# A mixture-of-experts stage reordered: one expert's row list inside its neighbour's inner product, both row turns between the outer products

## The chip, the cores and the metric

One Trainium2 chip, and of it one core. The metric is the device time of one launch in microseconds (us), shown as the median of three runs. Beside it stands one profiled execution, from which all rows below come. TensorE is called PE here, VectorE DVE, ScalarE ACT, GpSimd POOL and SyncE SP, as in the profile.

## What is computed

The reference is a two-layer model on 625 nodes with 768 features. Each layer adds to `x` a graph part and a feed-forward part, each on the layer norm of `x`:

```
x = x + gat(layernorm(x))                   # 10000 edges, 8 heads, then 1 head
x = x + moe_ffn(layernorm(x)) + spectral    # 8 experts, all of them on all rows
x = x + rgcn_and_gcn(layernorm(x))          # 34 relations, 768x768 weights each
x = x + routed_experts(layernorm(x))        # the stage that is changed
```

The last part is

```
logits = flat @ Wr;  probs = softmax(logits);  topk_p, topk_i = top_k(probs, 2)
capacity = ceil(625 * 2 / 8 * 1.25) = 196
order  = argsort(-score, axis=1)[:, :capacity]     # per expert: the 196 best rows
gate, up = silu(flat[order] @ w1), flat[order] @ w3          # 768 -> 192
out    = scatter_add((gate * up) @ w2 * weight) + silu(flat @ s1) * (flat @ s3) @ s2
```

so that there is one shared expert over all 625 rows (five tiles of 125) and eight routed experts with 196 rows each, in two halves of 98.

## The kernel before, in words

The kernel is one program with five queues that are written out by hand; every wait on a semaphore is in the text, and the order in a queue is the order of execution. Three stretches matter here.

**The relation stage.** For each of 34 relations a one-hot list (`in_list`, DVE) picks rows; PE turns the list into row numbers (`list_rows`), POOL gathers rows by them, PE turns the rows and multiplies them by the relation's weights, which ACT and DVE have split into a high and a low part (`w_high`, `w_low`). `in_list` of relation r+3 stands in the DVE queue of relation r, behind `w_low` of relation r+1; PE's `list_rows` of it stands ahead of the products of relation r+1.

**The shared expert.** PE makes five inner products (`shared_inner`; the first three carry eight more columns with the router's logits, and `last_logits` makes those of tiles 3 and 4 by themselves), turns the hidden rows (`shared_turn`) and makes five outer products (`shared_outer`). DVE adds each of these straight from PSUM to the residual `x_res` (`add_shared`), between pieces of its ranking work. ACT computes silu (`shared_gate`), the router's exp (`router(2)`) and the copies (`shared_turned`).

**The routed experts.** For expert e, in this order:

- PE spreads the scores of all rows over the partitions (`score_spread(e)`, five transposes into PSUM slot 3), ACT copies them out (`score_row(e)`), DVE ranks every row against them (`rank(e)`, with fourteen compare-and-sum instructions) and writes the one-hot list (`placed(e)`).
- PE multiplies the list by the row numbers (`list_places(e)`, ten narrow matmuls into slot 0), DVE reads the numbers (`rows2(e)`), POOL issues two gathers of 98 rows each from DRAM into `fx`.
- PE turns both halves (`turn_x(e, 0)` and `turn_x(e, 1)`, both into slot 0, so that the second waits until ACT's `take_x` has emptied it), makes the inner product in three parts of 12 matmuls (gate in two parts, then up), and two outer products of 8 matmuls (`outer_product(e, 0)` and `(e, 1)`), whose results ACT writes out (`y_out`) and stores to `y_dram`.
- SP loads the weights of expert e as soon as the inner product of expert e-3 (`w13`) and its outer products (`w2e`) are done, in a ring of three.

In the loop before, PE's queue for expert e from 2 on is: inner product e; first turn of e+1; first outer product of e; second turn of e+1; spread e+4; a wait for `x_taken` of both halves of e+1; `list_places(e+2)`; second outer product of e. So a row list is made two experts ahead of its use. `turn_hots(0)` and `turn_hots(1)`, which turn the last expert's one-hot list, come in the loop at experts 5 and 6.

**The end.** The rows of experts 0 to 5 that a node needs are gathered back from `y_dram` (`y_lower`) and added with their weights (`add_lower`, five DVE instructions, placed before the last expert's `hidden_rest`), those of a second choice likewise (`y_higher`, `add_higher`); the last expert's result is split in two parts (`y_last` on ACT, `last_low` on DVE) and multiplied by the one-hot lists (`join`, PE), DVE adds the result (five instructions), and SP stores each tile.

## Time and profile before

| | us |
|---|---|
| runs (three) | 1416.32, 1418.84, 1422.12 |
| median | 1418.84 |
| profiled execution, own time | 1422.75 |
| its span in the profile | 1421.2 |
| mean granted PE clock, share of full | 0.953 |
| PE busy in the span | 1303.6 (92%) |
| DVE busy | 964.3 (68%) |
| POOL busy | 649.2 (46%) |
| ACT busy | 557.1 (39%) |

The span is what the profiler saw of the one execution, some 1.6 us less than that execution's own time. Granted clock 1.00 is 2.4 GHz, 0.50 is 1.2 GHz. A busy PE is not PE at its peak: a stretch at the lower clock counts as busy too.

### The profile page before, as it was taken

What the parts mean: (1) busy time and instruction counts of PE and PEld (TensorE: products, weight loads), DVE (VectorE), ACT (ScalarE), POOL (GpSimd) and SP (SyncE); (2) the same over time, 40 slices, a digit from 0 to 9 for tenths busy, and PEclk for the clock granted to TensorE, in tenths of its full rate; (3) what the DMA queues carried; (4) which work ended last, traced back from release to release, by engine and by line L of the source; (5) the groups of instructions that cost most, each with busy time, mean ns of one, the idle gap of its engine ahead of it and who ended that gap; (6) DMA issues with size and microseconds to landing.
All of it is one profiled execution on the core that took longest, in us unless ns stands there. A gap on an engine that the chain in (4) does not pass through costs nothing.

```text
span 1421.2 us, 22852 instructions
## 1 busy us (share of the span) xinstructions
PE 1303.6 (92%) x7540; PEld 1103.8 (78%) x7540; DVE 964.3 (68%) x2158; ACT 557.1 (39%) x652; POOL 649.2 (46%) x564
## 2 busy tenths in 40 slices
PE   7988678999999989999999999999999879988997
PEld 5765568656996779999999999999866569656665
DVE  8967899888689645565656565656158875477634
ACT  0010476232433044555555555555147761212221
POOL 7025777767677633344434443544178740011121
PEclk9999697999999899999999999999999999989998
DMA  6940000020740347878787878787579863415645
GB/s 172 91 46 6 2 2 1 2 68 1 208 107 2 91 156 253 291 251 298 253 304 258 297 255 298 263 293 246 142 248 328 271 211 89 129 41 161 169 133 167
DMA packets 116402, 234.59 MB, mean 165 GB/s; under 512 B 36930, under 2 KB 57086, under 8 KB 116300
## 3 DMA queue, kind: packets, MB, share of 16 engines
q1 hardware_dynamic: 80780, 126.83, 31.0%
q0 software_dynamic: 22352, 70.40, 17.7%
q10 hardware_dynamic: 13200, 36.46, 6.9%
q8 instruction: 39, 0.64, 0.2%
q14 instruction: 31, 0.25, 0.1%
HBM read 195.26 MB, written 39.70 MB: 165 GB/s over the span
## 4 chain that ended last, share of the span: by engine, by line
PE 64%; DVE 21%; issue 5%; DMA 4%; ACT 3%; POOL 1%; DVEq 0%; ACTq 0%; SPq 0%; POOLq 0%
PE PS L2725 28%; PE PS L2599 4%; PE PS L2388 4%; PE PS L2713 3%; PE PS L3010 3%; PE PS L2674 3%; PE PS L2788 3%; DVE e L1321 3%; PE PS L2900 2%; PE PS L2999 2%; PE PS L2858 2%; DVE mlo L2163 2%; DVE e L1563 2%; DVE e L1600 1%; DMA pre<-z_dram,grow 1%
## 5 line engine op out<-in xcount | busy, mean ns | idle before, releaser
L815 POOL DMA_INDIRECT xg<-xn_dram,xrow x70 | 111.7, 1596 | 270.0 <-DVEq L1530 248.2
L2725 PE MATMUL PS<-whi,xhi 128*128 128x384 f32 x840 | 220.8, 343 | 1.0 <-ACTq L1103 1.0
L2725 PE MATMUL PS<-whi,xlo 128*128 128x384 f32 x840 | 215.0, 337 | 0.0
L2725 PE MATMUL PS<-wlo,xhi 128*128 128x384 f32 x840 | 213.5, 335 | 0.0
L1321 DVE TENSOR_TENSOR wlo<-raw,whi 128x2304 fp32r<-128x2304 f32 x68 | 175.2, 2576 | 39.6 <-ACTq L1086 33.7
L1084 ACT ACTIVATE whi<-raw 128x2304 fp32r<-128x2304 f32 x68 | 145.1, 2134 | 27.3 <-DMA raw<-in_L_gnn_W_rel 11.6
L2725 PEld LDWEIGHTS PS<-wlo,xhi 128*128 128x128 f32 x840 | 152.0, 188 | 0.0
L2725 PEld LDWEIGHTS PS<-whi,xlo 128*128 128x128 f32 x840 | 151.9, 188 | 0.0
L2725 PEld LDWEIGHTS PS<-whi,xhi 128*128 128x128 f32 x840 | 148.5, 189 | 1.3 <-issue 1.3
L1321 DVE TENSOR_TENSOR xlo<-PS,xhi 128x768 fp32r<-128x768 f32 x70 | 67.0, 958 | 121.6 <-ACTq L1095 114.3
L785 POOL DMA_INDIRECT zidxb<-zrow_dram,idxb x80 | 110.9, 1386 | 25.7 <-issue 25.7
L783 POOL DMA_INDIRECT evwb<-inv_dram,idxb x80 | 106.6, 1333 | 30.5 <-issue 22.4
L801 POOL DMA_INDIRECT edge_dram<-recb,idxb x80 | 97.1, 1214 | 39.5 <-issue 21.4
L1101 ACT ACTIVATE xn<-PS 128x768 f32<-128x768 f32 x70 | 56.8, 812 | 145.5 <-PE PS L2725 131.2
L1094 ACT ACTIVATE xhi<-PS 128x768 fp32r<-128x768 f32 x70 | 56.9, 813 | 86.6 <-issue 53.6
L2388 PE MATMUL PS<-onehot 125*128 125x347 bf16 (+6 forms) x640 | 74.8, 261 | 10.7 <-DVE onehot L1387 10.7
L884 POOL DMA_INDIRECT fx<-xn_dram,xrow x16 | 15.5, 971 | 141.1 <-DVEq L2251 138.6
L2388 PEld LDWEIGHTS PS<-onehot 125*128 125x128 bf16 x640 | 53.8, 99 | 27.4 <-issue 10.7
L2858 PE MATMUL PS<-mhi,hotf 128*125 128x384 f32 x170 | 59.7, 433 | 16.7 <-DVE mlo L2163 11.2
L2491 PE MATMUL PS<-hx,e 125*125 125x97 f32 x350 | 51.9, 323 | 15.2 <-DVE e L1600 15.2
L859 POOL DMA_INDIRECT pre<-z_dram,grow x45 | 56.7, 1260 | 16.8 <-issue 8.8
L2491 PEld LDWEIGHTS PS<-hx,e 125*125 125x125 f32 x350 | 51.0, 238 | 16.2 <-issue 16.2
(463 smaller groups left out, 2652.0 us busy)
## 6 DMA issues: line engine op xcount, KB each, us to landing
raw<-in_L_gnn_W_rel SPq DMA_DIRECT2D x68, 1152.0 KB
z_dram<-xn ACTq DMA_DIRECT2D x70, 384.0 KB, 7.3
gw<-in_L_gnn_W SPq DMA_DIRECT2D x2, 2304.0 KB, 27.1
fw<-in_L_ffn_w SPq DMA_DIRECT2D x8, 576.0 KB
fw<-in_L_ffn_w ACTq DMA_DIRECT2D x1, 4608.0 KB
y_dram<-yb ACTq DMA_DIRECT2D x14, 294.0 KB
xn_dram<-xn SPq DMA_DIRECT2D x10, 384.0 KB
wroot<-in_L_ffn_w SPq DMA_DIRECT2D x5, 576.0 KB, 4.9
```

Of the source, the lines that this page charges most:

```text
L783: pool.indirect_dma_start(evwb[:, n:n + 1], None, inv_dram, bass.IndirectOffsetOnAxis(ap=idxb[:, 0, n:n + 1], axis=0)).then_inc(evw_loaded ...
L785: pool.indirect_dma_start(zidxb[:, n:n + 1], None, zrow_dram, bass.IndirectOffsetOnAxis(ap=idxb[:, 1, n:n + 1], axis=0)).then_inc(rows_loa ...
L801: pool.indirect_dma_start(edge_dram, bass.IndirectOffsetOnAxis(ap=idxb2[:, k:k + 1], axis=0), recb[:, k, :], None, bounds_check=T * GE - 1 ...
L815: pool.indirect_dma_start(xg[b][j][:, :], None, xn_dram, bass.IndirectOffsetOnAxis(ap=xrow[:, b, j:j + 1], axis=0)).then_inc(x_gathered[b] ...
L1084: step.do(act.activation(whi[b][:, half * KH:(half + 1) * KH, :], raw[:, half * KH:(half + 1) * KH, :], ACT.Copy))
L1094: step.do(act.activation(xhi[b][j][:, :, :], columns_of(j), ACT.Copy))
L1321: return dve.tensor_tensor(o, a, b, op)
L2388: pe.matmul(PS[:, c:c + m], onehot[:, b, i * 128:(i + 1) * 128], onehot[:, b, HOT_REL + o:HOT_REL + o + m], start=start and c % BANK == 0, ...
L2491: mm = pe.matmul(slot(3)[0:P, b * BANK + i * (HC + 1):b * BANK + (i + 1) * (HC + 1)], e2[b][:, t, i * P:(i + 1) * P], hx[:, t, h * (HC + 1 ...
L2599: mm = pe.matmul(o[0:end, :, :], w[:, k, 0:end], xs[:, t0:t1, k, 0:TW], start=(k == 0 and part == 0), stop=(k == K - 1 and part == 2), ski ...
L2725: mm = pe.matmul(slot(q)[:, s * BANK:s * BANK + HALF], a[:, k, :], wt[:, k, s * HALF:(s + 1) * HALF], start=(k == 0 and part == 0), stop=( ...
L2858: mm = pe.matmul(slot(MSG_SLOT[n][0])[0:P, s * BANK:s * BANK + HALF], hotf[q % 4][:, 0:P], part[:, s * HALF:(s + 1) * HALF], start=False, ...
```

## The change

All changes are in the order of work, in two PSUM slots and in waits; the same sums are formed, the adds in another order.

- PE: `list_places(e+1)` is now made inside the inner product of expert e, between the gate parts and the up part; for every expert the queue is inner product, spread e+3, first outer product, both turns of e+1, second outer product. `turn_x(e, 0)` writes slot 0 and `turn_x(e, 1)` slot 3 (`X_SLOT`), and the waits for `x_taken` ahead of the turns and the list are gone. A row list is thus made one expert ahead, and a score row three ahead. Both `turn_hots` are in expert 6.
- DVE: `rank` and `placed` of expert n+2 behind `hidden_first(n)`; `add_shared` reads SBUF and is moved to after `row_tables`, `add_lower` to after the last `hidden_first`.
- ACT: copies the shared outer products out of PSUM (`shared_out`, into the buffer `xn`, once its five stores to DRAM have landed), and makes one exp of a column of ones ahead of the router's.
- PE, shared expert: the logits of tiles 3 and 4 behind `shared_inner(1)` and `shared_inner(2)`; `shared_outer(0)` ahead of the first spread.
- SP: the load of `w13` for expert e waits for the rows of expert e-2 as well.
- Relation stage: the one-hot list of relation 3 is made before the stage and not in its first turn.

```diff
-SPREAD_AHEAD = 4
+SPREAD_AHEAD = 3
+X_SLOT = (0, 3)
+SHARED_SLOT = (0, 1, 2, 1, 2)
...
             for e in range(RING, NE):
                 sp.wait_ge(inner_full, SH + 3 * (e - RING + 1))
+                for k in range((e - RING + 1) * RT, (e - RING + 2) * RT):
+                    sp.wait_ge(x_gathered[k % 4 // 2][k % 2], 16 * (REL // 2 + (k % 2 == 0) + k // 4 + 1))
                 load_w13(e, e % RING, ld_w13[e % RING])
...
+            def shared_out(t):
+                act.wait_ge(outer_full, t + 1)
+                step.do(act.activation(xn[:, t, :].rearrange("p (b c) -> p b c", b=2),
+                                       slot(SHARED_SLOT[t]).rearrange("p (b c) -> p b c", c=BANK)[0:P, :, 0:HALF], ACT.Copy))
+                act.sem_inc(outer_taken, 1)
+
             for t in range(LOGITS_WITH):
                 shared_gate(t)
+            act.activation(table_of_exp[:, :], ones[0:P, 0:1], ACT.Exp)
             shared_turned(0)
             router(2)
             shared_gate(3)
             shared_turned(1)
+            score_row(0)
+            act.wait_ge(xn_stored, 32 * T)
+            shared_out(0)
             shared_gate(4)
-            score_row(0)
             shared_turned(2)
+            shared_out(1)
             shared_turned(3)
+            shared_out(2)
             score_row(1)
+            shared_out(3)
             shared_turned(4)
-            score_row(2)
+            shared_out(4)
...
             for n in range(NE):
                 expert_gates(n)
+                if n == 0:
+                    score_row(2)
+                if n + SPREAD_AHEAD < NE:
+                    score_row(n + SPREAD_AHEAD)
+                if n == FINAL - 1:
                     for j in range(RT):
+                        hot_out(j)
...
                 y_out(n, 0)
+                for j in range(RT):
+                    take_x(n + 1, j)
                 y_out(n, 1)
...
-            in_list(2, 0)
+            for b in range(2):
+                in_list(2 + b, b)
...
             def add_shared(t):
+                dve.wait_ge(outer_taken, t + 1)
+                do(tt(x_res[:, t, :], xn[:, t, :], x_res[:, t, :], ALU.add))
...
+            for n in range(NE):
                 hidden_rest(n)
+                if n + 1 < NE:
+                    rows2(n + 1)
                 hidden_first(n)
                 if n + 2 < NE:
+                    rank(n + 2, 0, T)
+                    placed(n + 2)
+                elif n + 2 == NE:
                     row_tables()
+                    for t in range(T):
+                        add_shared(t)
...
+            dve.wait_ge(y_lower_gathered, 16 * T)
+            for t in range(T - 1):
+                add_lower(t)
+            last_low(0)
+            add_lower(T - 1)
             add_higher(0)
             last_low(1)
+            for t in range(1, T):
+                add_higher(t)
...
             def turn_x(e, j):
...
-                if k:
-                    pe.wait_ge(x_taken, k)
+                if j == 1 and e == FINAL:
+                    pe.wait_ge(hots_ready, RT)
+                elif j == 1:
+                    pe.wait_ge(srow_ready, min(e + SPREAD_AHEAD, NE) if e else 2)
...
+            for e in range(NE):
+                def between():
+                    if e + 1 < NE:
+                        list_places(e + 1)
+                    if e == 0:
+                        score_spread(2)
+                    if e == FINAL - 1:
+                        turn_hots(0)
+
+                inner_product(e, between)
                 if e + SPREAD_AHEAD < NE:
                     score_spread(e + SPREAD_AHEAD)
+                if e == FINAL - 1:
+                    turn_hots(1)
+                outer_product(e, 0)
+                if e < FINAL:
+                    for j in range(RT):
+                        turn_x(e + 1, j)
                 outer_product(e, 1, 0 if e == FINAL else 2)
```

## Rows read from the trace of the kernel before

**Rows 1.** Windows: stretch, length, busy by engine (instructions), clock, DMA share, GB/s

```profile
1266.90:1390.60 123.70, 110.15 (x553) 76.76 (x553) 67.29 (x295) 29.27 (x48) 18.31 (x19) 0.90 0.55 153
...
1342.75:1359.69 16.94, 15.42 (x76) 10.34 (x75) 9.89 (x43) 3.60 (x6) 1.94 (x2) 0.90 0.64 175
...
1376.90:1390.62 13.72, 13.55 (x70) 9.67 (x69) 1.04 (x4) 4.29 (x7) 4.75 (x5) 1.00 0.61 198
```

**Rows 2.** Timeline of PE, experts 4 to 6: start, us, line, idle before it

```profile
1349.60 2.99 PE L3010 MATMUL PS<-w2e,hidden 128*98 128x384 f32 x8
1352.52 0.72 PE L2985 MATMUL PS<-ident,fx 98*128 98x98 f32 x6
1354.66 0.62 PE L2965 MATMUL PS<-node_of,inlist 125*98 125x2 bf16 x10 [1.42 <-ACTq L1229]
1355.14 4.62 PE L3010 MATMUL PS<-w2e,hidden 128*98 128x384 f32 x8
1359.69 6.24 PE L2999 MATMUL PS<-fxT,wroot 128*128 128x196 f32 x36
...
1387.73 2.96 PE L3010 MATMUL PS<-pre,hidden 128*98 128x384 f32 x8
```

**Rows 3.** Windows around two falls of the clock, columns as in the first group

```profile
1232.60:1236.00 3.40, 3.40 (x7) 1.85 (x6) 1.46 (x9) 3.07 (x4) 0.00 (x0) 0.50 0.95 255
...
1355.50:1358.90 3.40, 3.40 (x6) 1.26 (x5) 3.02 (x13) 0.00 (x0) 1.94 (x2) 0.50 0.34 98
```

**Rows 4.** Timeline, row gathers of POOL and a weight load of SP

```profile
1259.49 0.97 POOL L884 DMA_INDIRECT fx<-xn_dram,xrow  x1 [0.30 <-issue]
...
1274.72 1.55 SPq L688 DMA_DIRECT2D pre<-in_L_ffn_w  x3
...
1356.10 0.97 POOL L884 DMA_INDIRECT fx<-xn_dram,xrow  x1 [14.70 <-DVEq L2251]
```

**Rows 5.** Chain that ended last: start, us, of two gathers up to landing

```profile
1276.05 6.79 DMA fx<-xn_dram,xrow
...
1397.32 5.01 DMA pre<-y_dram,yrow
```

**Rows 6.** Timeline of DVE: rank and list of expert 2; `row_tables`; first and last

```profile
1275.87 0.87 DVE L2227 TENSOR_SCALAR_CACHE_REDUCE compared<-srow,scol 125x625 f32<-125x625 f32 x1 [0.17 <-DVE xrow L2250]
...
1284.73 0.99 DVE L2242 TENSOR_SCALAR inlist<-iota,poscol 125x196 bf16<-125x196 int16 x5
...
1372.76 0.20 DVE L1321 TENSOR_TENSOR ysel<-asg,rev 125x40 f32<-125x40 f32 x1
...
1377.06 0.20 DVE L2289 TENSOR_REDUCE yw<-ysel 125x5 f32<-125x40 f32 x1
```

**Rows 7.** Timeline from behind the logits to the first inner product, all engines

```profile
1232.29 5.73 PE L2909 MATMUL PS<-pre,xT 128*125 128x384 f32 x12
...
1232.97 1.28 ACT L1025 ACT_TABLE_LOAD   x1
...
1241.94 0.71 PE L2426 MATMUL PS<-ident,scol 125*125 125x125 f32 x5
...
1247.99 2.06 DVE L1321 TENSOR_TENSOR x_res<-PS,x_res 125x768 f32<-125x768 f32 x2
...
1255.87 0.59 PE L2965 MATMUL PS<-node_of,inlist 125*98 125x2 bf16 x10 [1.91 <-DVEq L2244]
...
1266.89 7.80 PE L2999 MATMUL PS<-fxT,pre 128*128 128x196 f32 x36 [0.84 <-issue]
```

**Rows 8.** Timeline of PE and DVE, ahead of and in the relation stage

```profile
507.69 0.96 DVE L1321 TENSOR_TENSOR x_res<-PS,x_res 125x768 f32<-125x768 f32 x1 [5.92 <-PE PS L2695]
...
539.50 0.41 PE L2472 MATMUL PS<-node_of,inlist 125*128 125x2 bf16 x10 [2.97 <-DVEq L1513]
...
613.43 0.40 PE L2472 MATMUL PS<-node_of,inlist 125*128 125x2 bf16 x10 [1.32 <-DVEq L1513]
```

**Rows 9.** Timeline, the end: the last add

```profile
1414.39 1.02 DVE L2361 SCALAR_TENSOR_TENSOR x_res<-PS,comb,x_res 125x768 f32<-125x768 f32 x1 [0.39 <-PE PS L3076]
```

More of the change, by code:

```diff
@@ L1227, in take_x @@
                 act.wait_ge(turned, n * RT + j + 1)
-                step.do(act.activation(fxT[n % 2][:, :, j * HT:(j + 1) * HT], columns2(0)[:, :, 0:HT], ACT.Copy))
+                step.do(act.activation(fxT[n % 2][:, :, j * HT:(j + 1) * HT], columns2(X_SLOT[j])[:, :, 0:HT], ACT.Copy))
                 act.sem_inc(x_taken, 1)
@@ L2021, in x_low, with relation @@
                 dve.sem_inc(xlo_ready, 1)
-            def relation(i, b, listed, more):
+            def relation(i, b, listed, more, list_coming=True):
                 if more:
@@ L2030, in relation @@
                     w_low(i + b, 1 - b, 0, 1)
-                if listed:
+                if listed and list_coming:
                     in_list(i * 2 + b + 3, 1 - b)
@@ L2041, in _ @@
             for b in range(2):
-                relation(0, b, True, True)
+                relation(0, b, True, True, b == 1)
             with dve.Fori(1, REL // 2 - 2) as i:
@@ L2261, in hidden_first, with add_lower @@
                 dve.sem_inc(h2_ready, 1)
-            def add_lower():
-                dve.wait_ge(y_lower_gathered, 16 * T)
-                for t in range(T):
-                    step(dve.scalar_tensor_tensor(x_res[:, t, :], y_lower[t][0:P, :], yw[:, 0, t:t + 1], x_res[:, t, :], ALU.mult, ALU.add))
-                step.sync()
+            def add_lower(t):
+                do(dve.scalar_tensor_tensor(x_res[:, t, :], y_lower[t][0:P, :], yw[:, 0, t:t + 1], x_res[:, t, :], ALU.mult, ALU.add))
             def row_tables():
@@ L2294, in _ @@
             shared_hidden(3)
-            shared_hidden(4)
             dve.wait_ge(earlier_ready, 1)
             rank(0, 0, 3)
-            add_shared(0)
-            add_shared(1)
+            shared_hidden(4)
             rank(0, 3, T)
             placed(0)
-            add_shared(2)
             rows2(0)
-            rank(1, 0, 2)
-            add_shared(3)
-            rank(1, 2, 4)
-            add_shared(4)
-            rank(1, 4, T)
-            placed(1)
-            hidden_rest(0)
-            hidden_first(0)
-            rows2(1)
-            rank(2, 0, T)
-            placed(2)
-            rank(3, 0, 3)
-            hidden_rest(1)
-            rows2(2)
-            hidden_first(1)
-            rank(3, 3, T)
-            placed(3)
-            rank(4, 0, 3)
-            rows2(3)
-            rank(4, 3, T)
-            placed(4)
+            rank(1, 0, T)
+            placed(1)
             do(dve.tensor_copy(ident16[:, :], ident[0:P, 0:P]))
-            for n in range(2, NE):
-                if n == FINAL:
-                    add_lower()
+            for n in range(NE):
                 hidden_rest(n)
+                if n + 1 < NE:
+                    rows2(n + 1)
                 hidden_first(n)
-                if n + 3 < NE:
-                    rank(n + 3, 0, 3)
                 if n + 2 < NE:
-                    rows2(n + 2)
-                if n + 3 < NE:
-                    rank(n + 3, 3, T)
-                    placed(n + 3)
-                elif n + 3 == NE:
+                    rank(n + 2, 0, T)
+                    placed(n + 2)
+                elif n + 2 == NE:
                     row_tables()
+                    for t in range(T):
+                        add_shared(t)
             def add_higher(t):
@@ L2911, in shared_inner, with logits_alone @@
                 mm.then_inc(inner_full, 1)
-            def last_logits():
+            def logits_alone(t):
                 pe.wait_ge(free[3], BEFORE["slot3"][3])
-                for t in range(LOGITS_WITH, T):
-                    pe.wait_ge(xT_ready, XT_TURNED[5] + t + 1)
-                    c = (t - LOGITS_WITH) * NE
-                    for k in range(K):
-                        mm = pe.matmul(slot(3)[0:P, c:c + NE], xT[:, k, t * P:(t + 1) * P], s13[:, k, 2 * F:2 * F + NE],
-                                       start=(k == 0), stop=(k == K - 1))
-                mm.then_inc(full[3], 1)
+                pe.wait_ge(xT_ready, XT_TURNED[5] + t + 1)
+                c = (t - LOGITS_WITH) * NE
+                for k in range(K):
+                    mm = pe.matmul(slot(3)[0:P, c:c + NE], xT[:, k, t * P:(t + 1) * P], s13[:, k, 2 * F:2 * F + NE],
+                                   start=(k == 0), stop=(k == K - 1))
+                if t == T - 1:
+                    mm.then_inc(full[3], 1)
             pe.wait_ge(split_lo, 2 * REL + SPLITS1 + K // 2)
@@ L2932, in _ @@
                 shared_inner(t)
[L2933 removed]
+                logits_alone(t + LOGITS_WITH - 1)
             def shared_turn(t):
@@ L3016, in _ @@
             shared_turn(1)
-            shared_inner(4)
+            shared_outer(0, 0)
             pe.wait_ge(hT_ready, 2)
@@ L3026, in _ @@
             shared_outer(2, 2)
+            pe.wait_ge(outer_taken, 1)
+            list_places(0)
             pe.wait_ge(hT_ready, 4)
```

61 lines of the change are left out of this document (3 added, 58 removed).

## The prediction, as made before the changed kernel ran

> **What bounds the kernel now.** I read the windows by stage first, then the timeline of PE in the expert stage, then the other queues at the places where PE waits. Between the first expert's inner product (1266.9) and the last one's (1390.6) lie 123.7 us, of which PE is busy for 110.2, at a mean granted clock of 0.90 [rows 1]. So PE bounds the stage, but loses time in two ways: 13.5 us idle, and part of the busy time at 1.2 GHz.
>
> One expert in the middle takes 16.94 us; expert 6, where PE does not wait for a list, 13.72 [rows 1]. The timeline shows the difference. After the first outer product (2.99 us) and the second turn, PE idles for 1.42 us until ACT has taken both halves, makes the list, and then needs 4.62 us for the same eight matmuls that take 2.96 where there was no such wait [rows 2]. The granted clock in that stretch is 0.50, the lower of the two levels [rows 3]. This comes once in each of experts 2 to 5, and costs 1.4 + 1.65 = 3.1 us where the wait is 1.42.
>
> Before the first expert, a chain over DVE's ranking sets the pace: PE waits 1.91 us for the first list at 1255.87, and the first inner product begins at 1266.89 [rows 7].
>
> **The change, part by part.** I walk through the queues with the durations of the rows.
>
> *One expert in the steady state.* The inner product takes 6.24 us, with the list (0.48 from its start to the next start) 6.72 [rows 2]. The hidden rows need another 0.6 before the outer product can start (13.72 less 6.24, two outer products of 2.9 and three short steps leaves no more); there a turn was hidden, now the spread of 0.71 [rows 7] is. So the first outer product starts 7.3 after the inner one, the first turn at 7.3 + 2.92 = 10.25. A turn takes about 0.6 with what follows it: the second could start at 10.8, the second outer product at 11.4, the next expert at 14.3.
>
> The new wait is for rows, since the list is now made for the next expert. It starts at 4.1 (24 of 36 matmuls). From there to the first gather are 1.44 us (1354.66 to 1356.10) [rows 2, 4], and the second gather follows 1.3 later (0.97 and 0.30) [rows 4]. Landing: a gather of 125 rows took 5.01 from issue, one of 98 rows beside a weight load 6.79 [rows 5]. I take 5.0, since the weights now start behind the rows; bounds are 4.3 (an estimate: 98 of 125 rows, by the share of the time that scales) and 6.8. With 5.0 the second half lands at 4.1 + 1.44 + 1.3 + 5.0 = 11.8, PE waits 1.0 us ahead of the second turn, and the next expert starts at 11.8 + 0.56 + 2.92 = 15.3; with 4.3 it is 14.6, with 6.8 it is 17.1. I take 15.2. Behind that wait stand the second turn, the second outer product and the next inner product, so that each us of it is one of the stage.
>
> Does the clock stay up? Before the fall at 1355.5 PE had a turn (0.7), an idle of 1.42 and the narrow list (0.6) [rows 2, 3], 2.6 us between the wide products. Now the list lies between wide matmuls, and two turns with the wait between them are left, about 2.1 us. Expert 6, with a turn and the one-hot turn back to back, kept 1.00 [rows 1]. Mine lies between; I take no fall, and price it as rival A.
> The Trainium skill (TensorE: Matmul & The Clock Gate, Part 4: PE-mode transpose) says that a transpose does not count as PE work in the way that a matmul does. By that, two turns with a wait between them are one quiet stretch, and the sum would be that of rival A. No row here shows turns alone.
>
> *DVE.* Rank and list of one expert take 9.85 us (1275.87 to 1285.72) [rows 6]. They start at 7.7 and the list is wanted 4.1 into the next expert, 15.2 + 4.1 - 7.7 = 11.6 later: 1.8 us of slack, so no cost; past that each us is one of PE. The five `add_shared` (1.03 each [rows 7]) leave the ranking chain. They now stand behind the tables of expert 6 (4.5 us, 1372.76 to 1377.26 [rows 6]) and ahead of `hidden_rest(7)`: done at 7.7 + 4.5 + 5.2 = 17.4, needed at 15.2 + 2.5. Just hidden.
>
> *The way to the first expert.* (1) Behind the logits alone, 24 matmuls of 8 columns, the clock falls and the fourth tile's inner product takes 5.73 us; 3.4 of that at 0.50 cost 1.7 [rows 3, 7]. Split into two pieces between wide products, I expect no fall: -1.7. (2) The first spread, at 1241.94, now waits for an outer product (2.9) and not for an inner one (5.73 - 1.7 = 4.0): -0.9. (3) Two adds (2.06) leave the first ranking, a small product (0.4) comes in [rows 7]: -1.7. The first list is thus made at 1251.5 and not 1255.87. Behind it PE has a spread (0.7), two outer products (2.9 each; ahead of the second, 1.0 of waiting, because ACT's new `shared_out(3)` stands ahead of the copy that it needs) and two turns. The second gather, 3.6 after the list as before (1255.87 to 1259.49 [rows 4, 7]), lands 5.0 later at 1260.1; then a turn and ACT's take lead to the inner product at about 1261.8, against 1266.89: -5.1. With the clock falling as before it is -3.4. (4) The exp of ones puts the router's table load (1.28 us [rows 7]) ahead of the need; its result comes 1 us sooner, but the spread waits for PE. I count nothing.
> The Trainium skill (ScalarE: Activation LUTs, What ACT_TABLE_LOAD costs) gives about 2.66 us with the drain for a switch of tables. A load of that length would end about 1234, a us later than needed, still ahead of the spread.
>
> *The first expert* begins after two turns and an idle of over 1 us, as before, and I leave it the slow start (7.80 for 6.24 [rows 2, 7]): 15.2 + 1.6, and a few tenths for the second spread inside it, 17.0 us.
>
> From the first inner product to the last: 17.0 + 6 x 15.2 = 108.2, against 123.7 [rows 1]: -15.5.
>
> *SP's wait.* The weights for expert e+3 now start some 12 us into expert e and are wanted over 30 us later; 1.2 MB at the stage's mean of 153 GB/s [rows 1] are 8 us. No cost. It removes what stood around the 6.79: weights issued at 1274.72, the gather at 1276.05 [rows 4, 5].
>
> *The end.* DVE bounds it. From 6.9 after the last inner product's start it has 5 lower, 5 higher and 5 last adds at 1.0 to 1.05 and two low parts of 0.96: 24.4, against 24.8 (1390.6 to 1415.4) [rows 9]. The lower rows are now issued behind the tables of expert 6 and land some 5.9 into the last expert, just before 6.9. -0.4.
>
> *Relation stage.* PE waited 2.97 us for the one-hot list of relation 3 [rows 8], which is now there: at most -3.0. But the chain of weight load, split and list runs close behind PE, which waits for it again at 613.43, 1.32 us [rows 8], and PE's lead may be given back there. Bounds 0 and -3.0; I take -2.0. The extra `in_list` ahead of the stage, 2 to 3 us, is followed by a DVE idle of 5.92 [rows 8], which hides it.
>
> **Sum.** -5.1 - 15.5 - 0.4 - 2.0 = -23.0. The profiled execution took 1422.75 us, so 1399.8 by its own time; the median of the runs is 3.9 lower, and from there 1418.84 - 23 = 1396.
>
> **The rivals.**
>
> *A. The clock still falls once per expert.* For it speaks the 1 us wait between the turns; against it, that the list has left that stretch. 1.65 x 6 = +9.9, with 1.7 at the logits +11.6: 1406 to 1408. Chance 0.20.
>
> *B. The rows come late, and the kernel is slower than before.* Gather latency is now on PE's path. Over seven experts, with the falls of A, the gain left is 23 - 9.9 = 13.1; it is used up once the second half lands 1.9 us later than I take, 6.9 from issue (the row beside a weight load has 6.79 [rows 5]). If the stores of `y_out`, the tail of a weight load and the other half's gather stretch it to 8.5, the sum is +11: 1430. Against it: the load is issued behind the rows and is over before the next gather. Chance 0.05.
>
> *C. The gain is swallowed by other waits*: DVE's 1.8 us of slack is not there, ACT's longer queue holds the start, the relation part gives 0. Within 7 us of before, about 1415. Chance 0.07.
>
> My own case has 0.68, with a range of its own of 1389 to 1403: rows after 4.3 us give -4 more, a relation stage with all 3 us another -1, a fast first expert -1.6; the relation part at 0, the fall at the logits and rows after 5.5 us give +7. 0.5% of this time is 7 us, about what a measurement of this kernel can tell from no change. The range over the cases is 1389 to 1410. Faster by over 0.5%: 0.88; within it: 0.07; slower: 0.05.
>
> **What would show it.** Right: starts of inner products 15.2 us apart; no outer product of 4.6 us; 0.5 to 1 us of idle ahead of the second turn, put down to the DMA into `fx`; the first inner product 5 us earlier after the logits, and none of 5.7 us behind them; no wait at the list of relation 3. Wrong: a clock of 0.50 once per expert (A); waits above 2 us at the turns (B); PE waiting for DVE at the list inside the inner product, or for ACT in the shared part (C); a wait for a list near 570 us that takes back the relation part.

## The result, and the profile after

Four runs of the changed kernel beside four of the kernel before gave 1405.31 us (1399.95 to 1408.58) against 1419.62. The medians are 14.3 us apart; the ratio on record is 0.988, 95% interval 0.986 to 0.990, which is 17 us (14 to 20). A second set (e1 below, with its own runs of the kernel before) gave 0.9876 (0.9848 to 0.9903), its medians 18.7 us apart. The forecast was 1396, with a range of 1389 to 1410. The profiled execution took 1404.76 us, its span 1403.0, at a mean granted clock of 0.955. Of the runs below, one of the twelve of e11 took 3233 us, more than twice the others, and is not in its ratio.

First the windows of the expert stage after: from the first to the last inner product, expert 4, expert 5 (columns as in [rows 1]).

```profile
1268.30:1372.40 104.10, 101.71 (x558) 73.28 (x558) 66.97 (x284) 29.96 (x49) 16.46 (x17) 0.98 0.58 167
1326.34:1340.88 14.54, 14.36 (x81) 10.39 (x80) 10.05 (x44) 4.30 (x7) 1.94 (x2) 1.00 0.71 205
1340.90:1357.90 17.00, 15.42 (x75) 10.40 (x74) 12.05 (x54) 3.61 (x6) 1.93 (x2) 0.90 0.56 159
```

123.7 us have become 104.1. The idle of 13.5 us is down to 2.4, and the clock went from 0.90 to 0.98 [rows 1]. By expert, from one inner product's start to the next, they were 23.7, 17.4, 17.9, 16.9, 16.9, 17.2 and 13.7 us before, and are 14.7, 14.4, 14.4, 14.6, 14.5, 17.0 and 14.5. So 8.9 of the 19.6 us come from the first expert alone. Before, PE waited in it for the rows of expert 1, which landed 6.79 us after issue beside the weights [rows 5], and a slow outer product (4.50 us) came behind. This line is from the kernel before:

```profile
1282.88 1.24 PE L2985 MATMUL PS<-ident,fx 98*128 98x98 f32 x6 [4.58 <-DMA fx<-xn_dram,xrow]
```

The timeline of PE after shows expert 4 and the end of expert 5; the rows beside it are POOL's second gather and SP's next weights in expert 4.

```profile
1326.34 4.25 PE L2984 MATMUL PS<-fxT,wroot 128*128 128x196 f32 x24
1330.42 0.58 PE L2948 MATMUL PS<-node_of,inlist 125*98 125x2 bf16 x10
1330.86 2.24 PE L2984 MATMUL PS<-fxT,wroot 128*128 128x196 f32 x12
1332.93 0.71 PE L2409 MATMUL PS<-ident,scol 125*125 125x125 f32 x5
1333.68 2.99 PE L2995 MATMUL PS<-w2e,hidden 128*98 128x384 f32 x8
1336.61 1.59 PE L2970 MATMUL PS<-ident,fx 98*128 98x98 f32 x12
1338.03 2.92 PE L2995 MATMUL PS<-w2e,hidden 128*98 128x384 f32 x8
...
1352.87 1.06 PE L2970 MATMUL PS<-ident,fx 98*128 98x98 f32 x6 [1.00 <-DMA fx<-xn_dram,xrow]
1353.72 4.26 PE L2995 MATMUL PS<-w2e,hidden 128*98 128x384 f32 x8
```

```profile
1333.09 0.97 POOL L889 DMA_INDIRECT fx<-xn_dram,xrow  x1 [0.30 <-issue]
...
1337.50 1.80 SPq L691 DMA_DIRECT2D wroot<-in_L_ffn_w  x3
```

The list lies between wide matmuls, and of what stood between the outer products in [rows 2] only two turns are left, 1.59 us for 1.18 where no row was awaited (at 1265.55 below): a wait of 0.4. SP's load, which waits for the rows, starts 4.41 us after the second gather's issue, which I take for the landing. (Where PE waited for such rows in experts 0 to 4 of e5 to e8, its turn began 4.4 to 4.7 us after the issue.) Only in expert 5 does PE wait a whole 1.00 us, and there the outer product is slow (4.26). The chain that ended last has that gather:

```profile
1347.63 5.19 DMA fx<-xn_dram,xrow
```

Then the way to the first expert, PE's timeline, against [rows 7]. The shared part begins at 1219.36 here and at 1216.21 before, so 3.15 are to be taken off.

```profile
1235.44 4.04 PE L2892 MATMUL PS<-pre,xT 128*125 128x384 f32 x12
...
1254.32 0.96 PE L2948 MATMUL PS<-node_of,inlist 125*98 125x2 bf16 x10 [2.03 <-DVEq L2252]
1255.14 1.39 PE L2409 MATMUL PS<-ident,scol 125*125 125x125 f32 x5
1256.33 5.04 PE L2934 MATMUL PS<-pre,hhT 96*125 96x384 f32 x8
1261.20 0.38 PE L2924 MATMUL PS<-ident,shh 125*96 125x125 f32 x2
1262.87 2.85 PE L2934 MATMUL PS<-pre,hhT 96*125 96x384 f32 x8 [1.28 <-ACTq L1278]
1265.55 1.18 PE L2970 MATMUL PS<-ident,fx 98*128 98x98 f32 x12
```

The window around them (columns as in [rows 1]):

```profile
1254.00:1261.00 7.00, 6.68 (x23) 4.54 (x24) 3.88 (x16) 0.69 (x1) 1.98 (x2) 0.51 0.27 69
```

The list of expert 0 comes 4.7 us earlier in relation to the shared part. But behind it the clock falls to 0.51, the outer product takes 5.04 us, and PE waits 1.28 us for ACT. The first inner product (1268.27) gains only 1.8.

In the relation stage the list of relation 3 waits for nothing, and the next one for 2.03 us:

```profile
537.54 0.40 PE L2455 MATMUL PS<-node_of,inlist 125*128 125x2 bf16 x10
553.85 0.40 PE L2455 MATMUL PS<-node_of,inlist 125*128 125x2 bf16 x10 [2.03 <-DVEq L1524]
```

At the end of the kernel DVE waits for the gathered lower rows (`y_lower`) and starts its lower adds 8.5 us after the last inner product's start:

```profile
1380.93 3.12 DVE L2272 SCALAR_TENSOR_TENSOR x_res<-wroot,yw,x_res 125x768 f32<-125x768 f32 x3 [1.80 <-DMA fx<-y_dram,yrow]
```

By stages the two traces differ by: ahead of the relation stage + 1.2, relation stage - 2.4, message stage (from PE's last wait in the relation stage to the first product of the GCN; the same code in both) + 4.3, way to the first expert - 1.8, experts - 19.6, end 0.0 (30.6 us from the last inner product's start, in both). That is - 18.3; the spans differ by 18.2.

### The profile page after: what moved, and what is told of

Its sections match the earlier page's. It is cut to its first block, busy times and chain, and to the rows that moved or that the text cites. A ratio compares the mean times of both kernels' runs of the same rounds, so it can differ in the third digit from the quotient of the medians.

```text
span 1403.0 us, 22858 instructions
## 1 busy us (share of the span) xinstructions
PE 1297.3 (92%) x7540; PEld 1104.0 (79%) x7540; DVE 965.0 (69%) x2158; ACT 560.5 (40%) x658; POOL 640.8 (46%) x564
## 4 chain that ended last, share of the span: by engine, by line
PE 62%; DVE 21%; issue 8%; DMA 4%; POOL 2%; ACT 2%; DVEq 0%; SPq 0%; another core or an unknown queue 0%; ACTq 0%; POOLq 0%
PE PS L2708 30%; PE PS L2582 4%; PE PS L2371 4%; PE PS L2696 3%; PE PS L2520 3%; PE PS L2657 3%; PE PS L2771 3%; DVE e L1332 3%; PE PS L2883 2%; PE PS L2841 2%; DVE e L1574 2%; DVE e L1611 2%; DVE mlo L2175 2%; DMA pre<-z_dram,grow 1%; PE PS L2803 1%
## 5 line engine op out<-in xcount | busy, mean ns | idle before, releaser
L820 POOL DMA_INDIRECT xg<-xn_dram,xrow x70 | 107.1, 1530 | 282.8 <-DVEq L1541 249.8
L1089 ACT ACTIVATE whi<-raw 128x2304 fp32r<-128x2304 f32 x68 | 145.1, 2134 | 26.1 <-DMA raw<-in_L_gnn_W_rel 14.2
L788 POOL DMA_INDIRECT evwb<-inv_dram,idxb x80 | 108.7, 1359 | 30.5 <-issue 22.4
L806 POOL DMA_INDIRECT edge_dram<-recb,idxb x80 | 101.0, 1263 | 39.5 <-issue 22.5
L2841 PE MATMUL PS<-mhi,hotf 128*125 128x384 f32 x170 | 63.5, 458 | 17.1 <-DVE mlo L2175 15.5
L889 POOL DMA_INDIRECT fx<-xn_dram,xrow x16 | 15.5, 971 | 128.4 <-DVEq L2259 125.9
L2474 PE MATMUL PS<-hx,e 125*125 125x97 f32 x350 | 53.0, 327 | 16.9 <-DVE e L1611 16.9
L2474 PEld LDWEIGHTS PS<-hx,e 125*125 125x125 f32 x350 | 52.2, 243 | 17.9 <-issue 17.9
L2841 PEld LDWEIGHTS PS<-mhi,hotf 128*125 128x125 f32 x170 | 31.7, 210 | 43.7 <-DVE mlo L2175 29.6
```

The costliest lines, as they stand in the source:

```text
L788: pool.indirect_dma_start(evwb[:, n:n + 1], None, inv_dram, bass.IndirectOffsetOnAxis(ap=idxb[:, 0, n:n + 1], axis=0)).then_inc(evw_loaded ...
L806: pool.indirect_dma_start(edge_dram, bass.IndirectOffsetOnAxis(ap=idxb2[:, k:k + 1], axis=0), recb[:, k, :], None, bounds_check=T * GE - 1 ...
L820: pool.indirect_dma_start(xg[b][j][:, :], None, xn_dram, bass.IndirectOffsetOnAxis(ap=xrow[:, b, j:j + 1], axis=0)).then_inc(x_gathered[b] ...
L1089: step.do(act.activation(whi[b][:, half * KH:(half + 1) * KH, :], raw[:, half * KH:(half + 1) * KH, :], ACT.Copy))
L2474: mm = pe.matmul(slot(3)[0:P, b * BANK + i * (HC + 1):b * BANK + (i + 1) * (HC + 1)], e2[b][:, t, i * P:(i + 1) * P], hx[:, t, h * (HC + 1 ...
L2841: mm = pe.matmul(slot(MSG_SLOT[n][0])[0:P, s * BANK:s * BANK + HALF], hotf[q % 4][:, 0:P], part[:, s * HALF:(s + 1) * HALF], start=False, ...
```

## The experiments

Twelve kernels ran, in five rounds beside the kernel before: e1 to e4 on one chip, e5 to e8 on a second, e9 to e12 on a third. The kernel before is not equally fast on them (1411.8, 1421.4, 1422.0 us), so times are compared within a chip, and across chips only by ratio. "Start" is the time from the first inner product of the shared part to that of expert 0, "experts" that from the first to the last expert's inner product, both from the run's profile.

| run | median, before | ratio (95%) | start | experts |
|---|---|---|---|---|
| before | | | 50.7 | 123.7 |
| changed, first set | 1405.3, 1419.6 | 0.988 (0.986 to 0.990) | 48.9 | 104.1 |
| e1 the same | 1393.1, 1411.8 | 0.9876 (0.9848 to 0.9903) | 45.7 | 101.9 |
| e2 weights ahead | 1414.7, 1411.8 | 1.0030 (1.0006 to 1.0054) | 49.0 | 122.7 |
| e3 list late | 1429.8, 1411.8 | 1.0136 (1.0114 to 1.0158) | 47.4 | 139.4 |
| e4 relation old | 1395.0, 1411.8 | 0.9885 (0.9858 to 0.9911) | 49.0 | 101.4 |
| e5 logits together | 1406.1, 1421.4 | 0.9883 (0.9857 to 0.9910) | 47.3 | 102.4 |
| e6 adds in ranking | 1402.2, 1421.4 | 0.9869 (0.9843 to 0.9896) | 49.7 | 101.7 |
| e7 turned first | 1399.8, 1421.4 | 0.9841 (0.9816 to 0.9866) | 44.9 | 102.3 |
| e8 front | 1401.5, 1421.4 | 0.9844 (0.9819 to 0.9870) | 50.0 | 102.4 |
| e9 list in the middle | 1401.5, 1422.0 | 0.9853 (0.9816 to 0.9891) | 48.3 | 100.7 |
| e10 turn ahead | 1419.3, 1422.0 | 0.9982 (0.9958 to 1.0006) | 45.7 | 119.8 |
| e11 one slot | 1426.8, 1422.0 | 1.0023 (0.9991 to 1.0055) | 48.2 | 121.9 |
| e12 outer first | 1399.9, 1422.0 | 0.9845 (0.9808 to 0.9883) | 45.6 | 102.6 |

**e1, the changed kernel again.**

> The changed kernel once more, unaltered, as the measure for the runs beside it. In its first profile the experts from the first to the last inner product took 104.1 us, the first inner product came only 1.8 us earlier relative to the shared part, and the message stage, whose code is the same in both kernels, took 144.9 us against 140.6 before, at a clock of 0.91 against 0.96. If that is chance of the single execution, this profile has the message stage nearer to 141 and the ratio is 0.985 to 0.990; if the change itself slows that stage, it is near 145 again. Expert 5 alone was late (17.0 us for 14.5): if its place is chance, it moves or goes.

The code is that of the first profile, and start and experts differ all the same: the outer product behind the list took 2.75 us and not 5.04, and expert 5 waited 0.81 us without a slow outer product. The message stage took 162.1 us here, against 164.7 before and 169.0 in the first profile. Over all thirteen profiles of changed kernels it took 157.3 to 171.2, and it goes with the chip: 157.3 to 162.1 in e1 to e4, 164.6 to 167.1 in e5 to e8, 165.7 to 171.2 in e9 to e12. So the + 4.3 lies within what the same code shows on one chip (5.5 us in e9 to e12) and says nothing of the change; and most of the 10 us by which the first of these chips is faster lies in this stage.

**e2, the weights ahead of the rows.**

```diff
-                for k in range((e - RING + 1) * RT, (e - RING + 2) * RT):
-                    sp.wait_ge(x_gathered[k % 4 // 2][k % 2], 16 * (REL // 2 + (k % 2 == 0) + k // 4 + 1))
                 load_w13(e, e % RING, ld_w13[e % RING])
```

> The next weights are issued as soon as the inner product is over, as in the kernel before, and no longer behind the rows. My account: the load runs beside the gathers, which then land 6.8 us after issue (row of the kernel before) and not 4.5; PE waits about 2.4 us ahead of the turns of experts 1 to 5, the clock falls in the outer product behind (1.65 us each): + 10 to + 20 us against the changed kernel, ratio 0.995 to 1.002. Rival: the rows don't suffer from the load, and the wait is worth nothing: within 3 us of the changed kernel.

+ 21.7 us by the medians, just over the upper end, and the kernel is now 0.3% slower than before. In the profiles the experts account for + 20.8. Expert 2, PE and the second gather on POOL:

```profile
1302.08 0.72 PE L2968 MATMUL PS<-ident,fx 98*128 98x98 f32 x6
1305.48 1.24 PE L2968 MATMUL PS<-ident,fx 98*128 98x98 f32 x6 [2.68 <-DMA fx<-xn_dram,xrow]
1306.52 4.90 PE L2993 MATMUL PS<-w2e,hidden 128*98 128x384 f32 x8
```

```profile
1298.57 0.97 POOL L887 DMA_INDIRECT fx<-xn_dram,xrow  x1 [0.30 <-issue]
```

The rows are there 6.9 us after issue, as the row of before had it (6.79 [rows 5]). The five experts that issue a load took 18.6, 16.9, 19.5, 20.0 and 18.4 us, the two without one 14.8 and 14.6. The waits of those five are 2.2 to 2.7 us, as expected, and the clock fell behind three of them (outer products of 3.9 to 5.6 us). The rival falls: SP's wait, to which the prediction gave no gain of its own beyond the landing, is worth as much as the whole gain of the change (18.7 us on this chip), since without it the rest brings nothing.

**e3, the list behind the up part.** The only edit besides is that DVE's `rows2` follows `hidden_first`.

```diff
-                    if e + 1 < NE:
-                        list_places(e + 1)
...
                 inner_product(e, between)
+                if e + 1 < NE:
+                    list_places(e + 1)
```

> The list of the next expert is made behind the last part of the inner product and not ahead of it, so that its rows are asked for 2.1 us later. My account: the landing of the rows is on PE's path with next to no slack (0.1 to 0.4 us of waiting per turn), so each of seven experts loses about 2 us of waiting and, since the turns are then apart, the clock falls in the outer product behind them (1.65 us): + 14 to + 25 us against the changed kernel, ratio 0.998 to 1.006. Rival: there is slack, and PE's own work sets the 14.5 us of an expert: + 0 to + 4 us.

+ 36.8 us, more than I allowed. PE in expert 2:

```profile
1308.97 1.24 PE L2970 MATMUL PS<-ident,fx 98*128 98x98 f32 x6 [1.39 <-DMA fx<-xn_dram,xrow]
1310.98 1.24 PE L2970 MATMUL PS<-ident,fx 98*128 98x98 f32 x6 [0.77 <-DMA fx<-xn_dram,xrow]
1312.01 4.74 PE L2995 MATMUL PS<-w2e,hidden 128*98 128x384 f32 x8
```

The waits are 1.7 to 2.6 us an expert, about as expected. The clock's part is the larger one: 139.4 - 101.9 = 37.5 over seven experts is 5.4 each, so about 3 go to the lower clock. The outer product behind the turns is slow in all seven (3.9 to 5.6 us), and the next inner product in four of them (7.55 us at 1275.53, for 6.24).

**e4, the relation list as before.**

```diff
-            for b in range(2):
-                in_list(2 + b, b)
+            in_list(2, 0)
...
-                relation(0, b, True, True, b == 1)
+                relation(0, b, True, True)
```

> The one-hot rows of relation 3 are made inside the relation loop again, as in the kernel before; all else is changed. My account: + 2.4 us against the changed kernel, with the wait of 3 us ahead of the list of relation 3 back, and the later wait of 2 us gone. Rival: the later stages give the lead back, and it is within 1 us.

+ 1.9 us by the medians, within the intervals, so the times don't settle it. The trace is plainer: from the outer product before the stage (503.86 here, 503.44 in the kernel before) to the product behind PE's last wait in it there are 514.0 us, the same as in the kernel before (513.9), against 511.7 in e1 beside it and 508.9 to 513.8 in the twelve profiles with the new order at this place (mean 511.5). The first list waits 3.06 us again and the second not at all. How much the new order gains goes with its own second wait: where that was 0.6 to 1.4 us (e2, e6, e7, e9) the stage took 508.9 to 509.7, where it was 2.6 to 2.9 (e5, e8, e10, e12) 513.0 to 513.8.

**e5, the logits together.**

```diff
                 shared_inner(t)
-                logits_alone(t + LOGITS_WITH - 1)
+            for t in range(LOGITS_WITH, T):
+                logits_alone(t)
```

> The logits of the last two tiles stand together again, behind the third inner product of the shared part, as in the kernel before; all else is changed. My account: the clock falls behind the 24 narrow matmuls, the inner product of tile 3 takes 5.7 us and not 4.0, and the first inner product of the experts comes 1.7 us later: + 1.7 us against the changed kernel. Rival: DVE and ACT hold that stretch anyway, and the first expert is 0 to 0.5 us later.

The inner product behind the 24 narrow matmuls:

```profile
1241.65 4.04 PE L2892 MATMUL PS<-pre,xT 128*125 128x384 f32 x12
```

It took 4.04 us, as in the split order: the 5.73 us of [rows 7] did not come back. My account is not borne out. The same 24 matmuls together were followed by a fall in one profile and by none in the other, so what the split is worth is not shown; the ratio (0.9883 for 0.9876) can't tell 1.7 us from nothing.

**e6, the adds in the ranking.** `add_shared` reads PSUM on DVE inside the ranking, as in the kernel before, and ACT's `shared_out` is gone.

```diff
             rank(0, 0, 3)
             shared_hidden(4)
+            add_shared(0)
+            add_shared(1)
             rank(0, 3, T)
             placed(0)
+            add_shared(2)
             rows2(0)
-            rank(1, 0, T)
+            rank(1, 0, 2)
+            add_shared(3)
+            rank(1, 2, 4)
+            add_shared(4)
+            rank(1, 4, T)
```

> The five adds of the shared part read PSUM on DVE inside the first two rankings again, as in the kernel before, and ACT has no copies of it. My account: the list of expert 0 comes 2.1 us later, but PE's wait of 1.28 us for ACT's turned rows of tile 4 (behind the copy of tile 3 in the changed kernel) goes: + 0.8 us at the first inner product. By the reckoning of my prediction, which gave the adds 1.7 us and the copy 1.0 us of waiting, + 0.7 to + 2.1 us. Rival: the second ranking, now 2 us longer, makes the list of expert 1 late as well, + 3 us or more.

```profile
1250.53 0.96 PE L2950 MATMUL PS<-node_of,inlist 125*98 125x2 bf16 x10 [4.25 <-DVEq L2249]
1251.36 1.39 PE L2411 MATMUL PS<-ident,scol 125*125 125x125 f32 x5
1252.54 4.85 PE L2936 MATMUL PS<-pre,hhT 96*125 96x384 f32 x8
...
1258.12 2.85 PE L2936 MATMUL PS<-pre,hhT 96*125 96x384 f32 x8 [0.51 <-ACTq L1278]
```

The list is 2.2 us later (4.25 of waiting for 2.03), and 0.77 come back where PE waited for ACT. Against the profiles in which the clock fell as far, the start is 0.8 us longer (49.7 for 48.9 and 49.0). In the median nothing of it is seen.

**e7, ACT turns the rows of tile 4 before its copy; e8, besides, PE's second spread ahead of the first list.**

```diff
-            shared_out(3)
             shared_turned(4)
+            shared_out(3)
```

> ACT turns the hidden rows of tile 4 ahead of its copy of the shared output of tile 3. My account: the wait of 1.28 us ahead of the outer product of tile 4 goes, all or all but 0.3 us, and the first inner product of the experts comes 1.0 to 1.3 us earlier: - 1.0 to - 1.3 us. Rival: the rows of expert 0 (issued 3.6 us behind its list, landing 4.5 us later, so 8.1 us behind the list) are not there yet, and PE waits for them at the turns instead: 0 to - 0.3 us. From the trace: list at 1254.32, rows at 1262.4, turns at 1265.55, so there are 3 us of slack and I expect the first.

```diff
+            pe.wait_ge(hT_ready, 4)
+            score_spread(1)
             pe.wait_ge(outer_taken, 1)
             list_places(0)
-            pe.wait_ge(hT_ready, 4)
-            score_spread(1)
             shared_outer(3, 1)
```

> As the run with the turned rows of tile 4 first, and besides PE makes the spread of expert 1 ahead of the list of expert 0, in the 2.03 us in which it waits for that list. My account: the spread's 0.8 us leave the path behind the list, and the clock's fall behind that idle (outer product of 5.04 us in one profile, 3.2 in another) becomes rarer: first inner product - 1.8 to - 3.8 us against the changed kernel. Rival: the turned rows of tile 3, for which the spread waits, are late, or DVE is the bound up to the list and the clock falls as before: - 1.0 us, no better than the run beside it.

e7 has a wait of 0.51 for 1.28, and a start of 44.9 against the 45.7 of e1, where the clock held too: - 0.8. The rows of expert 0 are just there: the two turns take 1.24 us, without a wait, so the three microseconds of slack that I had counted on had been those of the slow outer product. In e8 the spread filled part of the wait, but the clock fell further, not less:

```profile
1250.31 0.71 PE L2409 MATMUL PS<-ident,scol 125*125 125x125 f32 x5
1252.50 0.74 PE L2948 MATMUL PS<-node_of,inlist 125*98 125x2 bf16 x10 [1.49 <-DVEq L2252]
1253.11 5.46 PE L2934 MATMUL PS<-pre,hhT 96*125 96x384 f32 x8
...
1259.50 5.48 PE L2934 MATMUL PS<-pre,hhT 96*125 96x384 f32 x8 [0.51 <-ACTq L1278]
```

Both outer products took 5.5 us. My account for e8, that the fall becomes rarer, has nothing for it in this profile; one profile can't refute it either.

**e9, the list in the middle of the gate part.** On top of e7's order:

```diff
                 for part, n, q, bank in INNER:
                     if part == "up":
-                        between()
+                        if not e:
+                            between()
...
                     for k in range(K):
+                        if e and part == "gate" and k == K // 2:
+                            between()
```

> With the turned rows of tile 4 first, as in the run of that name; and from expert 1 on the list of the next expert is made in the middle of the second part of the inner product, some 1.0 us earlier than in the changed kernel. My account: the rows land 1.0 us earlier, which removes the 0.1 to 0.4 us of waiting of each expert and the 0.4 to 2 us of expert 5, and experts come 14.3 us apart throughout: first to last inner product 100.5 to 101.5 us against 102 to 104, - 1 to - 2.5 us against the run with the turned rows first. Rival: DVE, which has the list ready 2.8 to 3.0 us into an expert, is late for a list at 3.1, and PE waits there what it saves: no change, or + 1 us.

```profile
1314.12 3.25 PE L2987 MATMUL PS<-fxT,pre 128*128 128x196 f32 x18
1317.27 0.62 PE L2948 MATMUL PS<-node_of,inlist 125*98 125x2 bf16 x10
1317.75 3.23 PE L2987 MATMUL PS<-fxT,pre 128*128 128x196 f32 x18
...
1324.49 1.23 PE L2970 MATMUL PS<-ident,fx 98*128 98x98 f32 x12
```

No wait is left, at the list or at the turns, and experts 1 to 5 take 14.32, 14.31, 14.32, 14.32 and 14.23 us. That is PE's own work in this order, and the waits of the changed kernel over it are 1.2 us in all by e1 (3.4 in the first profile, with the fall in expert 5). In the medians e9 can't be told from e7.

**e10, one turn ahead of the outer product (and ACT's copy of it ahead of `y_out`); e11, one slot for both turns.**

```diff
+                if e < FINAL:
+                    turn_x(e + 1, 0)
                 outer_product(e, 0)
                 if e < FINAL:
-                    for j in range(RT):
-                        turn_x(e + 1, j)
+                    turn_x(e + 1, 1)
```

> The first turn of the next expert stands ahead of the first outer product again, as in the kernel before, the second between the outer products; the list stays inside the inner product. My account: the first half's rows land some 10.0 us into the expert (first gather issued at 5.5, 4.5 to land) and the turn wants them at 7.0, so PE waits 2.5 to 3 us in each of seven experts, and the clock falls in the outer product behind: + 18 to + 32 us against the changed kernel, experts 17 to 19 us apart. Rival: with the list that early the rows are there for either place, and the place of the turn is worth under 3 us in all.

```diff
-X_SLOT = (0, 3)
+X_SLOT = (0, 0)
...
-                if j == 1 and e == FINAL:
-                    pe.wait_ge(hots_ready, RT)
-                elif j == 1:
-                    pe.wait_ge(srow_ready, min(e + SPREAD_AHEAD, NE) if e else 2)
+                if k:
+                    pe.wait_ge(x_taken, k)
```

> Both turns go through the same PSUM slot again, so that the second waits until ACT has taken the first; both stand between the outer products. My account: between the two turns PE idles for the copy (0.66 us) and the ways there and back, about 1.0 us, and the second outer product starts that much later: 15.3 to 15.6 us an expert, + 6 to + 9 us; if the clock falls behind the idle in some experts, 1.65 to 3 us each on top, up to + 25. Rival: the second half's rows land as late as that copy ends, so the wait is hidden in the wait for them: + 0 to + 2 us.

PE in an expert of e10, then of e11:

```profile
1307.33 0.71 PE L2409 MATMUL PS<-ident,scol 125*125 125x125 f32 x5
1310.24 0.73 PE L2970 MATMUL PS<-ident,fx 98*128 98x98 f32 x6 [2.19 <-DMA fx<-xn_dram,xrow]
1310.80 2.91 PE L2995 MATMUL PS<-w2e,hidden 128*98 128x384 f32 x8
```

```profile
1310.19 0.72 PE L2968 MATMUL PS<-ident,fx 98*128 98x98 f32 x6
1312.43 0.73 PE L2968 MATMUL PS<-ident,fx 98*128 98x98 f32 x6 [1.51 <-ACTq L1234]
```

Each costs nearly the whole gain or all of it: experts take 119.8 and 121.9 us. In e10 the wait is 1.3 to 2.5 us, and the clock fell in two of seven experts (18.3 us each; the others 16.4 to 16.9), so that the cost is below my range (+ 15 us by the ratios). In e11 the wait is 1.79 us in the first expert and 1.51 in the others, more than the 1.0 I gave it, and six of seven experts took 17.3 to 18.4 us, one 15.9. 14.3 + 1.5 is 15.8, so six had a stretch of the lower clock on top. The falls behind the wait are five, with outer products of 3.9 to 4.7 us; the sixth expert is slow because the fall in the one before it lasted into its inner product (5.77 us for 4.25). The cost (+ 21 us) lies near the upper end. Put back one at a time, the four pieces of e2, e3, e10 and e11 cost 21, 37, 15 and 21 us, together far more than the gain: each alone brings a wait per expert back, and falls of the clock with it, so these are no shares that could be added.

**e12, an outer product in the wait for the first list.** On top of e9, `list_places(0)` and its wait stand behind `shared_outer(3, 1)`.

> As the run with the list in the middle of the second part, and besides PE runs the outer product of tile 3 ahead of the list of expert 0, in the 2 us in which it waited for that list. In six profiles the clock fell behind this wait in five, by 1.7 to 5 us, and not in two. My account: the wait of 2.03 us is filled, the rows of expert 0 are asked for 1.0 us later and become the bound, landing 8.1 us behind the list at 44.1 us after the start of the shared part: the first inner product comes at 46 to 47 us, against 44.9 without and 48 to 50 with the fall: 0 to - 2 us against the run beside it. Rival: PE then idles 3 us for the rows, the clock falls there and takes the first inner product with it (7.8 us for 6.2, as in the kernel before): + 1 to + 3 us.

(The count in it is wrong: nine profiles with the change were there by then, and the clock had fallen at this place in seven of them.)

```profile
1259.43 0.73 PE L2970 MATMUL PS<-ident,fx 98*128 98x98 f32 x6 [1.55 <-DMA fx<-xn_dram,xrow]
1261.35 1.24 PE L2970 MATMUL PS<-ident,fx 98*128 98x98 f32 x6 [1.20 <-DMA fx<-xn_dram,xrow]
```

The start is 45.6 us, but the fall moved behind it, as the rival has it: the gate parts of the first inner product took 6.10 us for 4.22, and the first expert 16.6 for 14.7. Start and experts together are 148.2, with 147.2 in e7, 149.0 in e9, 147.6 in e1 and 153.0 in the first profile. No order of this part is shown to be better. e7, e8, e9 and e12 all stand near 0.985, and their intervals overlap that of the changed kernel.

## Why the prediction was right, and where it was off

The forecast's side and mechanism held, and the measured 1405 lies in its range, but 2 us outside the range of my own case and 9 above its centre. The terms, by the first profile and by the experiments:

- *Experts, - 15.5.* Measured - 19.6 with one fall, and 101.4 to 102.4 us, so - 21.3 to - 22.4, in e1 and e4 to e8, whose expert loop is the same. Mis-sized in two steps. Landing: 5.0 us taken, 4.4 measured (the lower bound was 4.3, scaled down from the 125 rows by a share that the prediction does not give), so that PE waits 0.1 to 0.4 us in most experts and not 1.0, and most are 14.2 to 14.8 us apart; the prediction had 14.6 for 4.3. The first expert: 14.7 us and not 17.0, since its inner product ran at full clock (4.22 and 2.16 us around the list). The prediction also laid the loss before on experts 2 to 5, at 3.1 us each, and left out the wait of 4.58 us in the first; the term did not suffer, because it was taken from the whole stage, but SP's wait, which removes that cause, got no share of the gain.
- *The way to the first expert, - 5.1.* Measured - 1.8, and - 1.7 to - 5.0 over the seven profiles that have this order, the first among them (mean - 3.0). The list came 4.7 us earlier, as reckoned (4.4). What failed is the step behind it: it let the four pieces behind the list run at full clock, though PE waits for that list as before. The clock fell behind this wait in seven of ten profiles with the same order. ACT's copy cost a wait of 1.28 us (1.0 foreseen), of which 0.77 goes when the copy is gone (e6) or stands behind (e7).
- *Of it, the split of the logits, - 1.7.* Not shown (e5).
- *Relation stage, - 2.0.* - 2.4, and - 2.5 in the mean; a second wait of 0.6 to 2.9 us took back part, as the prediction's last sentence feared.
- *End, - 0.4.* 0.0 in the span, but the step failed: the lower rows did not land 5.9 us into the last expert, DVE waited 1.80 us for them, started the lower adds at 8.5 and not 6.9, and ended its last add 25.5 us in, for 24.8 before; the stores behind it took that much less. In eleven of thirteen changed profiles DVE waited there, 1.4 to 2.9 us. Why they come late is open: three of POOL's five gathers took 1.7 us each to issue, for 0.95 before, but in e6, where none did, the rows landed no earlier (8.7 us). In e11, where the rows came in time, the last add ended at 24.5, as reckoned.
- *SP's wait at no cost.* Right, and e2 shows what it is worth in this order: 21 us.
- *Rival A, a fall per expert.* It came once in the first profile, behind a wait of 1.00 us, and not in e1 behind 0.81. The wait of over 1 us that it needed mostly did not arise, because the rows land sooner. The Trainium skill (TensorE: Matmul & The Clock Gate, Part 4: PE-mode transpose) says that a transpose does not count as PE work in the way that a matmul does. If that made the two turns a quiet stretch, rival A would have come with any wait; the traces do not bear that out: turns of 1.2 to 1.6 us in one piece, and thirteen pairs with a wait of 0.2 to 0.8 us between them (e1, e2, e4 to e8), left the outer product behind at 2.9. Where 1.5 to 1.8 us of waiting lay between the turns (e11), the clock fell in five of seven.
- *Rival B, late rows.* Not the case, but e2 is its test: rows 6.9 us after issue, the point from which I had the gain used up, gave a ratio of 1.003.
- *DVE's slack.* 1.8 us foreseen; in e1 the list is written at 1303.69 and read at 1304.97, 1.3 us. It was enough.
- *The exp ahead.* The router's result comes 0.9 us sooner, and nobody waits for it. The table load is 1.28 us again and the exp starts right behind it, so the Trainium skill's 2.66 us with the drain (ScalarE: Activation LUTs, What ACT_TABLE_LOAD costs) is not seen here.

In the first profile my terms sum to - 2.4 - 1.8 - 19.6 + 0.0 = - 23.8, against - 23.0 forecast: two sizes off by 3 to 4 us cancel. That the sum is near is luck in these two. That the runs differ by 14 to 17 us and not by 24 has other causes. The profile of before was 3.1 us above the median of its four runs, and the stage with the same code took 4.3 us more in the profile after. But with the means over the profiles that have the same code there (experts - 21.4, way to the first expert - 3.0, relation stage - 2.5) the stages promise some - 27 us; 17 are measured, 3.1 are the profile of before, and 6 to 7 are missing. The one profile of before has slow products at 1232.29 (5.73 us), 1257.32 (5.48) and 1266.89 (7.80, the first expert's inner product), and five slow outer products in the experts, where later profiles show such falls to come and go; if the kernel before mostly runs without some of them, that is the rest. This is argued, not shown: the kernel before was profiled once. So the sum of the medians came out in the range partly by luck: the stages gained more than forecast against this profile, and less of it stands against the median of the runs.

What also stays open is why PE's second turn in expert 5, where no weights are loaded, came 4.9 to 5.2 us after the gather's issue in four of the profiles with this loop (first profile, e1, e7, e8), and at most 4.6 in the other three.

## What to carry to other kernels

When two engines work in turns, put the request for the next data inside the longest block of work, and let the bulk load start behind the data that is awaited: here one semaphore wait on the loading queue decided 21 us. A wait of 1.3 to 2.7 us between short pieces of PE work cost its length here and, in 17 of 26 experts of e2, e3, e10 and e11, 1 to 4 us more through the clock. So move it next to long pieces or make it go, and count the falls in several profiles before a term rests on one of them. Take a sum from a single profiled execution as uncertain by at least that execution's distance from the median, and compare stages on one chip only.

## What the runs showed of the hardware

- The clock's fall is no function of the wait alone. With the same order and the same 2.03 us of idle, it fell in seven of ten profiles, with outer products of 4.0 to 5.3 us, and held in three, at 2.75. A wait of 1.9 to 2.5 us ahead of the first turn (e10) was followed by a fall in two of six experts, one of 1.51 us between two turns (e11) in four of six, one of 0.2 to 0.8 us between two turns in none of thirteen.
- A gather of 98 rows of 3 KB let PE's turn start 4.4 to 4.7 us after issue with the weight load behind it, and 6.7 to 7.0 us with the load beside it (e2).
- The same code took 157.3 to 162.1 us in the message stage on one chip and 164.6 to 171.2 on two others.
